# First V product split by chunks, x transposed in one place, Q's weights loaded earlier, last routing order

## The reference, cut to what matters

```python
n = layernorm(x)                                  # x: (8, 128, 512)
h = rmsnorm(n, ln_w)
q, k, v = h @ w_q.T, ctx @ w_k.T, ctx @ w_v.T     # 32 heads of 128, 8 batches of 128 tokens
a = softmax(q @ k.T + bias, masked) @ v
x = x + tanh(g0) * (n + a @ w_out.T)
n = layernorm(x)
top2 = two best of softmax(n @ w_router.T)        # 8 experts
x = x + tanh(g1) * (n @ W_base.T + b + sum over top2 of weight * (n @ A.T) @ B.T * 2)
```

## Time and profile before

| | us |
|---|---|
| median of 3 runs (857.56 to 858.68) | 858.48 |
| the profiled execution, its own time | 857.71 |
| its span (first to last instruction) | 855.9 |
| TensorE busy | 839.2 (98%) |
| VectorE busy | 534.7 (62%) |
| ScalarE busy | 454.4 (53%) |
| GpSimd busy | 163.7 (19%) |

### The profile page before, as it was taken

One profiled execution on the slowest core, in us unless ns is written; L12 is line 12 of the kernel. 1 busy time (PEld: TensorE's weight loads), 2 busy tenths in 40 slices (PEclk: granted clock), 3 DMA queues, 4 the chain that ended last, 5 costly groups with the idle time before them and its releaser, 6 DMA issues.

```text
span 855.9 us, 12491 instructions
## 1 busy us (share of the span) xinstructions
PE 839.2 (98%) x4402; PEld 713.0 (83%) x4402; DVE 534.7 (62%) x907; ACT 454.4 (53%) x1095; POOL 163.7 (19%) x135
## 2 busy tenths in 40 slices
PE   8899998989999999999999999999999999999998
PEld 7688886868888888888888888888888888888886
DVE  4775445657776777677767777777763454444445
ACT  5445556545666666666666666666764643330001
POOL 5544316401111111111111111112110000002210
PEclk9999999999999999999999999999999999999999
DMA  8364644282333432344244424443555766530001
GB/s 301 111 194 130 197 125 134 86 275 77 100 110 124 129 121 90 123 130 129 81 124 130 130 81 123 140 122 92 154 178 181 286 203 197 183 130 1 6 20 74
DMA packets 75933, 113.95 MB, mean 133 GB/s; under 512 B 5728, under 2 KB 40672, under 8 KB 75360
## 3 DMA queue, kind: packets, MB, share of 16 engines
q1 hardware_dynamic: 75872, 113.16, 41.5%
HBM read 77.48 MB, written 35.65 MB: 132 GB/s over the span
## 4 chain that ended last, share of the span: by engine, by line
PE 91%; DVE 3%; DMA 2%; ACT 2%; issue 2%; SPq 1%; POOL 0%; DVEq 0%; ACTq 0%; POOLq 0%
PE bank L273 73%; PE bank L1196 6%; PE bank L1179 6%; PE bank L1187 3%; DMA v_spill<-stage 1%; DVE wv L795 1%; PE bank L1091 1%; DMA raw_wo<-in_w_o 1%; ACT xs L612 1%; DVE cb L795 0%; DVE xb L795 0%; PE bank L1267 0%; PE bank L1126 0%; SPq L326 0%; ACT xb L571 0%
## 5 line engine op out<-in xcount | busy, mean ns | idle before, releaser
L273 PE MATMUL bank<-xb,wq 128*128 128x512 f32 x672 | 178.5, 401 | 2.4 <-DVE wq L795 2.2
L273 PE MATMUL bank<-cb,wq 128*128 128x512 f32 x672 | 177.9, 400 | 0.0
L273 PE MATMUL bank<-wo_hl,at_hl 128*128 128x512 f32 x768 | 177.9, 391 | 0.0
L273 PEld LDWEIGHTS bank<-wo_hl,at_hl 128*128 128x128 f32 x768 | 143.2, 188 | 29.3
L273 PE MATMUL bank<-wv,cb 128*128 128x512 f32 x672 | 157.7, 396 | 7.8 <-DVE stage L825 6.6
L273 PEld LDWEIGHTS bank<-wv,cb 128*128 128x128 f32 x672 | 127.7, 191 | 36.7 <-DVE wv L795 9.9
L535 POOL TENSOR_TENSOR bm<-bias_sb,mneg 128x512 f32<-128x512 f32 x64 | 74.6, 1166 | 404.0 <-DVE pr L909 385.5
L273 PEld LDWEIGHTS bank<-xb,wq 128*128 128x128 f32 x672 | 122.0, 189 | 26.2 <-DVE wq L795 2.6
L273 PEld LDWEIGHTS bank<-cb,wq 128*128 128x128 f32 x672 | 122.4, 189 | 23.3
L688 ACT ACTIVATE pr<-pr,nmax 128x128 f32<-128x128 f32 x256 | 99.2, 394 | 7.9 <-DVE nmax L911 7.9
L795 DVE TENSOR_TENSOR at_hl<-raw_at,at_hl 128x1024 fp32r<-128x1024 f32 x32 | 39.2, 1225 | 73.9 <-ACT wo_hl L704 73.7
(11 more groups left out here) (138 smaller groups left out, 980.3 us busy)
## 6 DMA issues: line engine op xcount, KB each, us to landing
v_spill<-stage SPq DMA_DIRECT2D x64, 256.0 KB, 3.5
raw<-in_w_qk SPq DMA_DIRECT2D x32, 512.0 KB, 5.4
v_sb<-v_spill SPq DMA_DIRECT2D x64, 256.0 KB, 3.2
at_spill<-at_sb SPq DMA_DIRECT2D x64, 256.0 KB, 2.8
raw_at<-at_spill SPq DMA_DIRECT2D x32, 512.0 KB, 3.9
raw_v<-in_w_v SPq DMA_DIRECT2D x16, 512.0 KB, 5.3
raw_wo<-in_w_o SPq DMA_DIRECT2D x32, 256.0 KB, 4.8
tok<-in_ctx_t SPq DMA_DIRECT2D x4, 512.0 KB, 7.1
```

Source lines behind the costliest of these rows:

```text
L273: mm = pe.matmul(dst, a, b, start=first and n == 0, stop=last and n == total - 1, skip_group_check=True)
```

## The change

- The context and weights of V's first product are loaded and split in two chunks of 128 rows of the contraction, 256 KB a load; the first product runs all four tiles over chunk 0 and then over chunk 1. WARM_UP is 30.
- The first token sum and first weight sum are made by VectorE (after iteration 0's split) and not by GpSimd.
- x is scaled after (1, 2) and (1, 4) into two buffers (eight batches); both transposes run inside and right behind the last product of group 1. The moments of the second half move from (1, 3) to (1, 1).
- x is split at one pair per product from (2, 1) to (3, 0); GpSimd's order of sums changes with it.
- Q's weights and bias are loaded ahead of the stores of M7 in group 3, and VectorE does `wq_lo(0), wq_lo(1)` ahead of the sums.
- At the end `routing(3)` stands before `finish(2)`, and `base(7)` is cut in two around `hw_transposes(3)`.

The diff, cut to its core:

```diff
-WARM_UP = 50
+WARM_UP = 30
-X_SPLITS = ((0, 1), (2,), (3,), (4, 5), (6,), (), ())
+X_SPLITS = {(2, 1): (0,), (2, 2): (1,), (2, 3): (2,), (2, 4): (3,), (2, 5): (4,), (2, 6): (5,), (3, 0): (6,)}
 # memory: xs1, four more batches, in the place of later xb
-            sb("x_pad0", [P, 11 * 2048], on=first)
+            sb("x_pad0", [P, 9 * 2048], on=first)
+            xs1 = sb("xs1", [P, HALF, D], on=first)
+            sb("x_pad2", [P, 2048], on=first)
 # SyncE
-            load_ctx(0, 0)
-            load_wv(0, 0, 0)
+            for c, b_in, a_in in ((0, b11_in, a11_in), (1, ctx_in[0, 0], wv_in[0][0])):
+                sp.dma_start(ctx_raw[:, 0, c, :], ctx_t[0, :, c, :]).then_inc(b_in, 16)
+                sp.dma_start(first_wv(c), w_v[0:2, :, 2 * P * c:2 * P * c + 2 * P].rearrange("k p n -> p k n")).then_inc(a_in, 16)
...
                     load_wv(g + 1, 1, 0)
-                store_v(g, M7)
-                if more:
-                    sp.wait_ge(sv_ok, 4 * g + 4)
-                    sp.wait_ge(wv_lo_ok, NP * g + 2)
-                    load_wv(g + 1, 0, 1)
                 else:
                     sp.wait_ge(xb_lo_ok, NP)
                     load_wq(0)
                     load_wq(1)
                     load_bias(0)
                     load_bias(1)
+                store_v(g, M7)
+                if more:
+                    sp.wait_ge(sv_ok, 4 * g + 4)
+                    sp.wait_ge(wv_lo_ok, NP * g + 2)
+                    load_wv(g + 1, 0, 1)
 # GpSimd
-            pool.wait_ge(ctx_in[0, 0], 16)
-            pool.wait_ge(ctx_in[0, 1], 16)
-            token_sum(1, ctx_q, ct_ok, cb_lo_ok)
-            wv_sum(0, 1)
...
-            for n in range(1, 5):
-                wv_sum(2, n)
-            wv_sum(3, 1)
-            wv_sum(3, 2)
+            wv_sum(2, 1)
+            wv_sum(2, 2)
             pool.wait_ge(xf_ok, 2 * DC)
             pool.wait_ge(xr_used, B)
             token_sum(1, x_q, xt_ok, xb_lo_ok)
             token_sum(2, x_q, xt_ok, xb_lo_ok)
+            wv_sum(2, 3)
+            wv_sum(2, 4)
+            token_sum(3, x_q, xt_ok, xb_lo_ok)
+            wv_sum(3, 1)
+            wv_sum(3, 2)
+            token_sum(4, x_q, xt_ok, xb_lo_ok)
             wv_sum(3, 3)
-            token_sum(3, x_q, xt_ok, xb_lo_ok)
             wv_sum(3, 4)
-            token_sum(4, x_q, xt_ok, xb_lo_ok)
 # ScalarE, after its part of the first product by chunks (128x512 each)
-                if i == 0 and g in (2, 3):
-                    transposed_tokens(g - 2)
...
-                v_copies(v)
+                if (g, i) == (1, NP - 1):
+                    v_copies(v, (0,))
+                    transposed_tokens(0)
+                    v_copies(v, (1, 2, 3))
+                else:
+                    if (g, i) == (2, 0):
+                        transposed_tokens(1)
+                    v_copies(v)
...
-                if (g, i) == (1, 3):
+                if (g, i) == (1, 2):
                     act.wait_ge(cb_lo_ok, NP)
                     scale_tokens(0)
-                if (g, i) == (2, 3):
+                if (g, i) == (1, 4):
                     scale_tokens(1)
 # VectorE
+            def first_sums():
+                ve.wait_ge(ctx_in[0, 1], 16)
+                ve.tensor_tensor(tt[0], ctx_q(0, 1), ctx_q(0, 0), ALU.subtract).then_inc(ct_ok, 1)
+                ve.wait_ge(wv_in[1][0], 16)
+                ve.wait_ge(wv_in[1][1], 16)
+                ve.tensor_tensor(sv[:, 0, :, :], raw_v_q(1, 0), raw_v_q(1, 1), ALU.add).then_inc(sv_ok, 1)
...
+                if v == 0:
+                    first_sums()
                 v_sums(v)
...
-                if (g, i) == (1, 3):
+                if (g, i) == (1, 1):
                     ve.wait_ge(x_in[1], 16)
...
+            wq_lo(0)
+            wq_lo(1)
             for n in range(1, 4):
                 wq_sum(0, n)
...
             hwt_lo(2)
+            routing(3)
             finish(2)
-            routing(3)
 # TensorE
+            def first_product():
+                for c, b_ok, a_ok, n in ((0, early_lo_ok, early_lo_ok, 2), (1, cb_lo_ok, wv_lo_ok, 1)):
+                    pe.wait_ge(b_ok, n)
+                    pe.wait_ge(a_ok, n)
+                    for t in range(HALF):
+                        mm = three_passes(pe, ps_va[t][:, :], [((cb[M1][:, 0, c, cols(t)], cb[M1][:, 1, c, cols(t)]),
                                                                (wv[:, 0, 0, c, :], wv[:, 0, 1, c, :]))],
                                          first=c == 0, last=c == 1)
                        if c == 1:
                            mm.then_inc(v_prod, 1)
...
-                        if g >= 2:
-                            pe.wait_ge(xf_ok, DC * (g - 1))
+                        if g == 2:
+                            pe.wait_ge(xf_ok, DC + t + 1)
...
+                if v == 2 * NP - 1:
+                    v_product(v, (0,))
+                    token_transposes(0)
+                    v_product(v, (1, 2, 3))
+                    token_transposes(1)
...
             base(6)
-            base(7)
+            base(7, (0, 1))
             hw_transposes(3)
+            base(7, (2, 3))
             up(3)
```

More of the change, by code:

```diff
@@ L633, in wq_hi @@
                 act.activation(wq[:, u % WRING, 0, :, :], wq_source(p, m), ACT.Copy).then_inc(wq_hi_ok, 1)
-            token_hi(0, ctx_q, cb, ct_ok, cb_hi_ok, ctx_in)
-            wv_hi(0)
+            for c, b_in, a_in, hi_b, hi_a in ((0, b11_in, a11_in, early_hi_ok, early_hi_ok),
+                                              (1, ctx_in[0, 0], wv_in[0][0], cb_hi_ok, wv_hi_ok)):
+                act.wait_ge(b_in, 16)
+                act.activation(cb[M1][:, 0, c, :], ctx_raw[:, 0, c, :], ACT.Copy).then_inc(hi_b, 1)
+                act.wait_ge(a_in, 16)
+                act.activation(first_split(0, c), first_wv(c), ACT.Copy).then_inc(hi_a, 1)
             for v in range(NP * GROUPS):
@@ L850, in _ @@
                     ve.tensor_reduce(allowed[:, :], mask8[:, :, :], AX.X, ALU.max).then_inc(allowed_ok, 1)
-                if g == 3:
-                    for n in X_SPLITS[i]:
-                        token_lo(n, x_q, xb, xb_hi_ok, xb_lo_ok)
+                for n in X_SPLITS.get((g, i), ()):
+                    token_lo(n, x_q, xb, xb_hi_ok, xb_lo_ok)
             ve.wait_ge(allowed_ok, 1)
@@ L928, in o_lo @@
                     lo(wo_hl[q % ORING][:, 1, h, :], raw_wo[:, h, :], wo_hl[q % ORING][:, 0, h, :]).then_inc(o_lo_ok, 1)
+            wq_lo(0)
+            wq_lo(1)
             for n in range(1, 4):
                 wq_sum(0, n)
-            for u in range(WRING):
-                wq_lo(u)
+            wq_lo(2)
+            wq_lo(3)
             wq_sum(0, 4)
@@ L1091, in _, with v_product @@
                 pe.transpose(ps_vd[3][:, 0:P], ident[:, :], ident[:, :])
-            def v_product(v):
+            def first_product():
[4 more added lines that the diff above has]
+                        mm = three_passes(pe, ps_va[t][:, :], [((cb[M1][:, 0, c, cols(t)], cb[M1][:, 1, c, cols(t)]),
+                                                                (wv[:, 0, 0, c, :], wv[:, 0, 1, c, :]))],
+                                          first=c == 0, last=c == 1)
+                        if c == 1:
+                            mm.then_inc(v_prod, 1)
+            def v_product(v, tokens=range(HALF)):
                 g, i = divmod(v, NP)
@@ L1098, in v_product @@
                     pe.wait_ge(cb_lo_ok, i + 1)
-                for t in range(HALF):
+                for t in tokens:
                     if m == M1 and g:
@@ L1125, in token_transposes @@
                     for c in range(DC):
-                        last = pe.transpose(ps_vd[c][:, cols(n)], xs[:, n, cols(c)], ident[:, :])
+                        if h and n == 0:
+                            pe.wait_ge(xf_ok, c + 1)
+                        last = pe.transpose(ps_vd[c][:, cols(n)], (xs, xs1)[h][:, n, cols(c)], ident[:, :])
                     last.then_inc(xr_used, 1)
-            for g in range(GROUPS):
-                for i in range(NP):
-                    v_product(NP * g + i)
-                if g in (1, 2):
-                    token_transposes(g - 1)
+            first_product()
+            for v in range(1, NP * GROUPS):
+                if v == 2 * NP - 1:
[3 more added lines that the diff above has]
+                    token_transposes(1)
+                else:
+                    v_product(v)
             def product(n):
@@ L1280, in lora, with base @@
                 mm.then_inc(lora_ps, 1)
-            def base(t):
+            def base(t, chunks=range(DC)):
                 pe.wait_ge(x1t_lo_ok, t + 1)
-                three_passes(pe, ps_x1[t][:, :], [(tok1, (base_hi[:, c, :], base_lo[:, c, :])) for c, tok1 in enumerate(tokens1(t))],
-                             last=False)
+                three_passes(pe, ps_x1[t][:, :], [(tokens1(t)[c], (base_hi[:, c, :], base_lo[:, c, :])) for c in chunks],
```

(1 more changed line is left out.)

31 lines of the change are left out of this document (20 added, 11 removed).

## The result

| | before | after |
|---|---|---|
| median of 6 runs (range) | 858.44 (857.56 to 860.12) | 852.94 (851.19 to 854.50) |
| the profiled execution | 857.71 | 853.30 |
| its span | 855.9 | 851.5 |

The ratio is 0.9933, with a 95% interval of 0.9916 to 0.9949: the change is faster by 5.5 us. The forecast was 9.6 us, a time of 848.9; the measured median, 852.94, lies just at the upper end of the range, 852.9. The sign was right, the size somewhat over half.

The account below looks back on a forecast made before the run. TensorE was busy 839.2 of 855.9 us, so only idle or lower-clock time could be won. Start 3.0, group 3 1.5, Q 4.2 and end 0.9 made 9.6 off 857.71: 848.1, as a median 848.9; range 844.7 to 852.9.

Parts of the forecast that it names:

- Start … Gain 2 to 3.4; I take 3.0: Group 0 of V: chunked first loads and earlier sums bring M7 forward from 36.96, gaining 3.0 us.
- I stay with the rate of the queued loads, since they overlap: Start: smaller loads keep the queued rate, 0.69 us for 256 KB, so the gain stays 3.0, not about 1.
- M5 at 19.8 … M7 at 33.6: Group 0, if VectorE goes first: M5 begins at 19.8 us, M7 at 33.6, before at 36.96.
- the first four loads go at half the rate, 2.7 more on everything behind: Start: worst case for loads of 1 KB rows; slow small loads as a rival gave 850.9, chance 0.13.
- TensorE starts at 6.8 and not at 9.49: Start: chunk 0 and thirty transposes are ready by 6.7, so V's first product begins at 6.8 us.
- the start does nothing for M7, since GpSimd's chain hangs on the eighth load, which does not move: Rival for group 0: start gain 0, time 851.9, chance 0.11.
- x in one place … 0.28 gained, once: Groups 1 and 2: scaling x after M7 of group 1 removes one of two 0.28 us holes.
- the slower rival: Group 2: splits wait for GpSimd's sums, 5.6 us lost a step over three steps; time 865.7, chance 0.05.
- V ends at 148.3 or 149.3 plus 27.4, I take 176.3: Group 3: sums and splits meet, M2 2.5 late, M5 3.2 late; V ends at 176.3 against 177.77, gain 1.5.
- my first rival: Group 3: the meeting of sums and splits does not happen or is hidden; V ends at 172.5, time 845.1, chance 0.15.
- Q's weights … 4.2: Q's first products: loading ahead of M7's stores removes the holes of 2.18 and 0.22 and 1.87 of slow clock, 4.2.
- End … 0.9: Kernel's end: routing(3) before finish(2) and a halved base(7) remove the 0.93 us idle before the last up.

Follow-up runs that it names:

- experiment 1: Changed kernel with the weights of V's first product in one 512 KB load with rows of 2 KB, not two of 256 KB; 850.55 us, ratio 0.9912 to the kernel before.
- experiment 6: Changed kernel with WARM_UP at 50 transposes in place of 30; 850.98 us, ratio 0.9914 to the kernel before.
- rows2k: The kernel of experiment 1: changed kernel with V's first weights in one load with rows of 2 KB; 850.55 us, ratio 0.9912.
- sums_on_gpsimd: Changed kernel with the first token sum and first weight sum back on GpSimd; 851.70 us, ratio 0.9922 to the kernel before.
- tail_undone: Changed kernel with the end in the old order: finish(2) ahead of routing(3), base(7) in one piece; 852.92 us, ratio 0.9943 to the kernel before.
- Experiment 2: Changed kernel with GpSimd's fourth x sum ahead of the two weight sums of group 3; 847.93 us, ratio 0.9888 to the kernel before.
- Experiment 3: Changed kernel with Q's loads behind the stores of M7 and wq_sum ahead of wq_lo, x splits still early; 854.84 us, ratio 0.9958 to the kernel before.
- turns: Changed kernel with two waits added on GpSimd, holding back sums until the weight splits of M6 and M7 are done; 850.49 us, ratio 0.9909 to the kernel before.
- sum4_early: The kernel of Experiment 2: changed kernel with GpSimd's fourth x sum moved ahead of two weight sums of group 3; 847.93 us, ratio 0.9888.
- warm_50: The kernel of experiment 6: changed kernel with 50 transposes in place of 30; 850.98 us, ratio 0.9914.
- experiment 4: The run of tail_undone: changed kernel with the end's old order restored; 852.92 us, ratio 0.9943 to the kernel before.

## Why the prediction was right or wrong

**"What bounds the kernel now"**: right in that nothing but holes and half clock was at stake, but the idle time as a whole stayed: 16.7 before (855.9 - 839.2), 16.5 after. Of the 4.2 by which TensorE's busy time fell, 2.75 are the transposes left out at the start (7.97 to 5.22), which came back as holes; the rest is rows that no longer run at half clock.

**"Start … Gain 2 to 3.4; I take 3.0"**: wrong, 0. The step that failed first is "I stay with the rate of the queued loads, since they overlap". The loads in rows of 1 KB cost some 1.9 us on every load behind (experiment 1), and "M5 at 19.8 … M7 at 33.6" hung on the seventh and eighth loads at 13.3 and 14.6, which were used at 15.25 and 16.57. What I called the bound, "the first four loads go at half the rate, 2.7 more on everything behind", was nearer than my value. Here the Trainium skill, page "DMA: Bandwidth & Descriptors", section "Bandwidth", warned in the right direction: by it I had the gain at about 1, an estimate, and two loads of 256 KB were slower than one of 512 KB (experiment 1). The rule that I drew on speaks of the size of a load. Here the size alone is not what costs: the context's two loads of 256 KB, in rows of 2 KB, stayed in experiment 1.

The chain as far as M6 stood. With the loads back it came as written: M5 at 19.68 (19.8), M6 at 27.98 (28.1). The second step that failed is from M6 to M7, "M7 at 33.6", a full-speed product behind M6. With the loads back M7 was at 35.05 (73.70 less the 38.65 from 36.96 to 75.61), by the clock behind the hole of 2.58, which I had charged behind M5 alone. In the changed kernel M6 ran at full clock, but the split of M7's weights met a further sum, which I had not counted: GpSimd's fourth token sum was issued at 32.45, the split at 33.50 took 3.41, and a hole of 1.25 opened. From M5 to M7 it is 15.3 there and 15.4 in experiment 1, where I had 13.8. So of the 3.4 by which M7 missed 33.6, 1.9 are the loads and 1.5 this step.

**"TensorE starts at 6.8 and not at 9.49"** was nearly right (7.20) and of no value: experiment 6 gives 1.2 of it back and loses nothing. My sum did not rest on it. The rival "the start does nothing for M7, since GpSimd's chain hangs on the eighth load, which does not move" (851.9, chance 0.11) had the number but not the reason: the eighth load did move, by 1.9, and in experiment 1, where it does not, M7 comes 1.9 earlier.

**"x in one place … 0.28 gained, once"**: right. **"No hole opens" in group 2**: right; the slower rival never came near.

**"V ends at 148.3 or 149.3 plus 27.4, I take 176.3"**: the mechanism was right, to the sums: 1, 2, then 4, with M2 0.8 late instead of 2.5 (VectorE came first, by 0.05 us; where GpSimd did, in `rows2k` and `sums_on_gpsimd`, M2 was 2.9 and 2.5 late) and M5 later by 3.04, in all 3.8 where I had 3.2. M5 began at 148.91, and 27.4 from there is 176.3, my figure. But behind this hole the clock halved again (28.84 for 27.4), and I had charged the clock only behind M2. Mis-sized term: 1.5 forecast, 0.2 measured, and the difference is this clock, which the execution of `tail_undone` did not pay (27.49). Experiment 2 shows that the hole before M5 is the fourth sum's place; the sentence "the order of sums 1, 2 and then 4 holds either way", in my first rival, named the line to move.

**"Q's weights … 4.2"**: right, 4.3 for the change as a whole. Its reason was half: I took the wait as that of `wq_lo` for the loads. Experiment 3 shows a second one behind it, M4's copies waiting for stores that stand behind Q's loads, which takes over as soon as the loads are a little early. And undoing the order alone lost 1.9 in the medians and 3.9 in its trace, so between 0.4 and 2.4 of the 4.3 belong not to the order but to the rest of the change, most likely to the splits of x that come earlier (not shown by a run of its own).

**"End … 0.9"**: right, 1.1 in the trace.

**Not foreseen:** the hole at 649, 1.0.

With the start at 0, group 3 at 0.2 and the new hole, the sum is 0.0 + 0.2 + 4.3 + 1.1 - 1.0 = 4.6, for spans 4.4 apart and medians 5.5. That the time came out at the edge of the range is due to Q's term and the end's; the other two won next to nothing.

## What to carry to other kernels

Before cutting a load into smaller ones to start sooner, look at what stands behind it: the work that sets the time may hang on the last load of the queue, and here halves with shorter rows delayed all of it. When two engines share a lock, list for each sum who reads it and when; one moved ahead of its turn, or one held back by a wait until the urgent splits are done, was worth 2 to 5 us here. And allow for a half clock behind each hole of 2 to 3 us, not only the first, as a range: it was 0 to 2.9 us behind the same hole in six executions.

## What the runs showed of the hardware that was not expected

- One load of 512 KB in rows of 2 KB was used at 5.33, the first half of the same data in rows of 1 KB at 5.70 and the second at 7.84.
- One instruction fetch of 16 KB in a load's flight went with 1.4 us more for 256 KB, in eight profiles of twelve and in no other.
- Two waits that were added made the kernel faster by 2.2 to 2.5 us in the medians, 2.6 in the trace of `turns`.
- A split that was issued 0.11 us ahead of GpSimd's sum took 1.22, one issued 0.23 behind it 3.25, and M5 of group 0 began at 19.42 in the one execution and at 22.32 in the other.
- TensorE's clock behind holes: after the idle of 2.33 at 21.68 and of 3.04 at 148.91 the granted clock was 0.54 and 0.53, near the 1.2 GHz level, in the windows that follow:

```profile
22.00:24.00 2.00, 2.00 (x7) 1.55 (x6) 2.00 (x4) 0.81 (x1) 2.00 (x2) 0.54 0.77 220
...
150.00:152.00 2.00, 2.00 (x7) 1.57 (x6) 1.76 (x2) 0.15 (x1) 0.75 (x2) 0.53 0.96 282
```

Behind the holes of 0.47 to 1.25 in the same stage no product took longer than 5.8. The length of a hole alone does not decide it: behind holes of 1.83 (`sum4_early`) and 1.84 (`warm_50`) M5 of group 0 took 7.33, behind one of 2.42 (`tail_undone`) 5.70, and behind the 3.04 of `tail_undone` the granted clock stayed at 1.00 (experiment 4).
